# Adding the key bias on GpSimd instead of by a matmul, with GpSimd's batch laid out in steps

## What is computed

```python
xn = layernorm(x)
Q, K, V = xn @ Wq.T + bq, xn @ Wk.T + bk, xn @ Wv.T + bv
Q, K = elu(Q) + 1, elu(K) + 1
KV = einsum('bshd,bshe->bhde', K, V);  K_sum = K.sum(axis=1)
Z = 1 / (einsum('bshd,bhd->bsh', Q, K_sum) + 1e-6)
out = einsum('bshd,bhde,bsh->bshe', Q, KV, Z) @ Wo.T + bo
return x + out + ffn(xn)
```

## Time and profile before

| | us |
|---|---|
| median of three runs | 1902.34 (1901.63 to 1903.81) |
| the profiled execution, its own time | 1900.01 |
| its span, first to last instruction | 1898.3 |
| PE busy | 1863.2 (98%) |
| DVE busy | 1300.6 (69%) |
| ACT busy | 1272.2 (67%) |
| POOL busy | 1026.2 (54%) |

### The profile page before, as it was taken

The page is one execution under the profiler, slowest core; times in us unless marked ns, Lnnn a source line. Parts: engine busy times, 40 slices in busy tenths (PEclk is TensorE's granted clock), DMA queues, the critical chain, the costliest instruction groups (busy, mean ns, idle before and its releaser), DMA issues. The chain is left out here.

```text
span 1898.3 us, 38991 instructions
## 1 busy us (share of the span) xinstructions
PE 1863.2 (98%) x13562; PEld 1269.6 (67%) x13562; DVE 1300.6 (69%) x2611; ACT 1272.2 (67%) x2045; POOL 1026.2 (54%) x947
## 2 busy tenths in 40 slices
PE   6899999999999999999999999999999999999998
PEld 4566666666676666666666666666666666666666
DVE  6678999998857777655787875555555555555556
ACT  6988887777746666666666666666666666666664
POOL 5656565656445555654455455545554554555453
PEclk9999999999999999999999999999999999999999
DMA  6979897989675555666677667576766766676857
GB/s 174 231 221 247 216 251 240 225 236 254 190 191 132 122 120 123 148 179 150 165 157 181 154 158 183 135 177 151 192 152 160 169 143 180 155 187 154 183 120 223
DMA packets 448900, 338.22 MB, mean 178 GB/s; under 512 B 224757, under 2 KB 430330, under 8 KB 448762
## 3 DMA queue, kind: packets, MB, share of 16 engines
q1 hardware_dynamic: 383674, 253.84, 48.5%
q0 software_dynamic: 48864, 66.88, 19.8%
q10 hardware_dynamic: 16224, 15.73, 2.5%
HBM read 185.61 MB, written 100.40 MB: 151 GB/s over the span
## 5 line engine op out<-in xcount | busy, mean ns | idle before, releaser
L1961 PE MATMUL pY<-w2s,hid 128*128 128x256 f16 x6144 | 756.6, 273 | 0.8 <-DVE hid L1806 0.8
L1946 PE MATMUL pH<-xgT,w1s 128*128 128x512 f16 (+1 forms) x3120 | 747.7, 376 | 1.3 <-PEq L324 1.3
L1961 PEld LDWEIGHTS pY<-w2s,hid 128*128 128x128 f16 x6144 | 599.8, 98 | 180.6 <-DVE yo L1822 3.6
L1806 DVE SCALAR_TENSOR_TENSOR hid<-gel,cur,hid 128x512 f16<-128x512 f32 (+1 forms) x520 | 384.6, 740 | 446.4 <-ACT hid L1745 440.8
L1720 POOL DMA_INDIRECT acc<-yo,idx x254 | 405.9, 1598 | 523.0 <-DVE yo L1822 450.0
L1742 ACT ACTIVATE gel<-pH,cur 128x512 f32<-128x512 f32 (+1 forms) x520 | 353.8, 680 | 476.7 <-PE pH L1946 457.2
L1946 PEld LDWEIGHTS pH<-xgT,w1s 128*128 128x128 f16 x3120 | 305.1, 98 | 252.4 <-DMA xgT<-xg 1.6
L1745 ACT ACTIVATE hid<-gel,cur 128x512 f16<-128x512 f32 (+1 forms) x520 | 372.0, 715 | 17.1
L219 POOL DMA_INDIRECT xg<-table,idx x256 | 286.1, 1118 | 112.1 <-issue 58.2
L1270 PE MATMUL pP<-wkv,xT 128*128 128x512 f16 x768 | 201.8, 381 | 7.8 <-DVE bias_rows L981 4.7
L724 POOL TENSOR_SCALAR xm<-xring,moments 128x256 f32<-128x256 f32 x128 | 120.9, 954 | 72.3 <-DVE xhl L1002 72.2
(11 more groups left out here) (236 smaller groups left out, 1888.5 us busy)
## 6 DMA issues: line engine op xcount, KB each, us to landing
stage<-in_w SPq DMA_DIRECT2D x160, 512.0 KB, 6.4
xring<-in_x SPq DMA_DIRECT2D x16, 1024.0 KB, 6.4
x2ring<-in_x SPq DMA_DIRECT2D x16, 1024.0 KB, 7.6
table<-xhl SPq DMA_DIRECT2D x32, 512.0 KB, 4.1
mix<-x2ring SPq DMA_DIRECT2D x32, 512.0 KB, 3.0
acc<-zeros SPq DMA_DIRECT2D x16, 1024.0 KB, 4.6
fmix<-mix SPq DMA_DIRECT2D x48, 256.0 KB, 3.5
facc<-acc SPq DMA_DIRECT2D x48, 256.0 KB, 4.0
```

The source lines that it names most:

```text
L1806: v.scalar_tensor_tensor(out=hid[:, hc % 4, 1, w], in0=gel[:, hc % 2, w], scalar=cur[expert_of(b, q)][:, 1:2], in1=hid[:, hc % 4, 0, w], o ...
L1946: last = t.matmul(pH[hc % 4][:, tok], w[:, aw, c, hc * P:(hc + 1) * P], xgT[i][:, ad, c, tok], start=k == 0 and c == 0, stop=k == 2 and c ...
L1961: last = t.matmul(pY[s // 2][:, s % 2, :], hid[:, hc % 4, ad, s * P:(s + 1) * P], w[:, aw, hc, :], start=hc == 0 and k == 0 and s % 2 == 0 ...
```

## The change

The product L1273 is left out for tiles 0 to 6 of each batch and kept for tile 7. A new constant `bk_all` holds the key bias in all partitions, made once by a product into `pG` and an ACT copy. For tiles 0 to 6, `keys` only copies the bank into `kv1`; POOL then adds `bk_all` to the keys there (`add_bk`, event `k_biased`); after that ACT makes `ek` from `kv1` (`key_exp`, relu and exponential), at the end of its step. POOL's list of a batch is written in eight steps that begin with `add_bk(n, j)`. DVE's list is unchanged. `bo_row` moves into a free part of `x2ring`, and the making of two constants is split off (`spread_consts`).

```diff
+            bk_all = sb("bk_all", [P, D], F32)
...
+                def add_bk(n, j):
+                    if n == 0 and j == 0:
+                        pool.wait_ge(whi, at(whi, 0, 6))
+                    pool.wait_ge(kv_done, at(kv_done, n, j))
+                    g.tensor_tensor(kv1[:, j % 4, 0:DC, 0:P], kv1[:, j % 4, 0:DC, 0:P],
+                                    bk_all[:, :].rearrange("p (c t) -> p c t", c=DC), ALU.add).then_inc(k_biased, 1)
...
                 for n in range(NB):
-                    for j in range(HALF, NT):
-                        centre(n, j)
-                    if n >= LAG:
-                        for u in range(4):
-                            add_bo(n - LAG, u)
-                    if n < NB - 1:
-                        norm(n + 1)
-                        for j in range(HALF):
-                            centre(n + 1, j)
-                    if n == 0:
-                        later_consts()
-                    if n + 1 >= LAG:
-                        blocks_of(n + 1 - LAG)
+                    s2, nxt = n >= LAG, n < NB - 1
+                    for j in range(NT):
+                        if n == 0 and j < HALF:
+                            centre(0, HALF + j)
+                        if j < NT - 1:
+                            add_bk(n, j)
+                        if s2 and j < 2:
+                            add_bo(n - LAG, 2 * j)
+                            add_bo(n - LAG, 2 * j + 1)
+                        if nxt and j == (3 if n == 0 else 2):
+                            norm(n + 1)
+                        if nxt and j == 3:
+                            for i in range(HALF - 1):
+                                centre(n + 1, i)
+                        if nxt and j == 4:
+                            centre(n + 1, HALF - 1)
...
+                        if n + 1 >= LAG and j == 4:
+                            scale_bv(n + 1 - LAG)
+                        if n + 1 >= LAG and j == 5:
+                            blocks_of(n + 1 - LAG)
+                        if nxt and j > 5:
+                            centre(n + 1, 2 * j - 8)
+                            centre(n + 1, 2 * j - 7)
...
+                def key_exp(n, j):
+                    if j < NT - 1:
+                        act.wait_ge(k_biased, at(k_biased, n, j))
+                        act.wait_ge(k_done, at(k_done, n, j - 2))
+                        a.activation(ek[:, j % 2, :].rearrange("p (c t) -> p c t", c=DC), kv1[:, j % 4, 0:DC, 0:P],
+                                     ACT.Relu, scale=-1.0).then_inc(kneg_done, 1)
...
-                            if k == 0 and c == 0:
+                            if j == NT - 1 and k == 0 and c == 0:
```

More of the change, by code:

```diff
@@ L350, in block_program @@
             bqT = sb("bqT", [P, DC], F32)
-            bo_row = sb("bo_row", [1, D], F32)
+            bo_row = x2ring[0:1, 1, 2, :]
             rows_all = sb("rows_all", [P, 2 * D], F32)
@@ L445, in block_program @@
             bias_step = event("bias_step")
+            k_biased = event("k_biased", per=NT - 1)
             lhs_done = event("lhs_done")
@@ L737, in blocks_of @@
                         g.tensor_scalar(kvm[:, c, :], bv_all[:, c * P:(c + 1) * P], kvs[:, c, P:P + 1], None, ALU.mult).then_inc(kvb_done, 1)
+                def blocks_of(m):
+                    kvs = kvring[:, m % QR, :, :]
                     for c in range(DC):
@@ L754, in _ @@
                 for n in range(NB):
[L755 to L767 removed]
+                    s2, nxt = n >= LAG, n < NB - 1
[14 more added lines that the diff above has]
+                            centre(n + 1, HALF - 1)
+                        if n == 0 and j == 4:
+                            later_consts()
+                        if n == 0 and j == 5:
+                            spread_consts()
+                        if n + 1 >= LAG and j == 4:
[5 more added lines that the diff above has]
+                            centre(n + 1, 2 * j - 7)
                 for u in range(4):
                     add_bo(NB - LAG, u)
+                scale_bv(NB - 1)
                 blocks_of(NB - 1)
@@ L792, in weights_high @@
                     a.activation(rows_all[:, :], pKV[:, :], ACT.Copy).then_inc(whi, 1)
+                    a.activation(bk_all[:, :], flat(pG)[:, 0:D], ACT.Copy).then_inc(whi, 1)
                 def high(n, j):
@@ L805, in keys @@
                     act.wait_ge(proj, at(proj, n, j))
-                    act.wait_ge(k_done, at(k_done, n, j - 2))
-                    a.activation(ek[:, j % 2, :], pP[j % 2][:, 0:D], ACT.Relu, scale=winv_neg[:, 2:3]).then_inc(kneg_done, 1)
+                    if j == NT - 1:
+                        act.wait_ge(k_done, at(k_done, n, j - 2))
+                        a.activation(ek[:, j % 2, :], pP[j % 2][:, 0:D], ACT.Relu, scale=winv_neg[:, 2:3]).then_inc(kneg_done, 1)
                     act.wait_ge(kv_used, at(kv_used, n, j - 4))
@@ L863, in _ @@
                         keys(n, j)
+                        if j == NT - 1:
+                            key_exp(n, j)
                         if nxt and j == NT - 2:
@@ L1258, in _ @@
                 pe.wait_ge(b_in, at(b_in, 0, 6))
+                t.matmul(flat(pG)[:, 0:D], ones[0:1, :], bias_raw[0:1, 0:D], start=True, stop=True)
                 t.matmul(pKV[:, 0:D], ones[0:1, :], bo_row[:, :], start=True, stop=True)
```

5 lines of the change are left out of this document (4 added, 1 removed).

## The result

The changed kernel takes 2002.76 us (median of 4 runs, 2000.92 to 2004.91), the kernel before 1902.74 beside it (1901.63 to 1903.81): ratio 1.0528, 95% interval 1.0515 to 1.0541. The profiled execution took 2000.92, its span is 1999.1 us, 100.8 longer than before. By the last `denominators` of the attention stage (625.47 us against 525.73) 99.7 of it have arisen.

What follows compares the result with a forecast made beforehand. The prediction took PE as the bound, with next to no slack between division and output. It added 69 us (batches 2 to 14), 1 (batch 15) and 10 (batches 0 to 2) to 1900.01: 1980 us, range 1945 to 2010.

Steps and rivals of the forecast that it cites:

- What the change removes, 12 us: On PE, 112 fewer bias products at 0.10 to 0.11 us: 0.75 us a batch, if PE never waits longer.
- The add, 0.75: On POOL, each 128x256 add taken as 0.75 us, between bounds 0.46 and 1.36; 5.3 us a batch fit POOL's room.
- Startup: Before the batches, one small product and ACT copy, taken as nothing; batches 0, 1 and 2's late begin together: 10 us.
- The walk: Batch 8's chain through POOL, ACT, DVE and PE: output starts 5.6 us late, rounded to 5.3 a batch; chance 0.59.
- I count it apart, as a rival: DVE stopped by POOL's SBUF reads, left out of the chain because the lost time would fall into DVE's idle time.
- no edge of this kind is left: From `output(m, 0)` to the next batch, 14.5 us of PE work: adds of tiles 5 and 6 have over 5 us.
- once 1.31: DVE's 32-element subtraction, median 0.22 us, took 1.31 once, just when POOL's `add_bo` of 1.36 began.
- The second: Rival: full chain, and PE's clock falls in its waits, slowing output work; 1.5 us a batch, 2000 us; chance 0.14.
- The fourth: Rival: DVE becomes the bound, each add blocking it for 0.75; period 33.8 us, time 1926 to 1930; chance 0.03.
- The first: Rival: shorter chain, ACT and POOL reach tile 2 no later; output 3.2 us late, 1945 us; chance 0.15.
- third: Rival: PE stays the bound, both divisions end by 278.2 in batch 8, whole 12 us gained: 1888 us; chance 0.07.
- fifth: Rival: no change within 0.2%, a wait that happens to cost just the gain; chance 0.02.

Runs made afterwards that it cites:

- run 3: The kernel before without the bias product for tiles 0 to 6 and nothing in its place, their key bias left out: 1893.34 us, ratio 0.9962.
- run 12: The changed kernel with two POOL memsets, still waited for, in place of each add; key bias of tiles 0 to 6 left out: 1991.82 us, ratio 1.0465.
- run 11: The kernel before, product kept, POOL's list in steps, with two memsets that nobody waits for in each add's place: 1924.63 us, ratio 1.0121.
- run 8: The changed kernel with logits and divisions earlier on DVE, POOL's list by due times, and ACT's tile 4 `ek` ahead of its `rstd` wait: 1948.66 us.
- run 9: As run 8, with DVE's root, second query feature and top-k parts 1 to 4 moved behind the divisions: 1923.54 us, ratio 1.0119.
- run 5: The changed kernel with `norm` of the next batch moved from step 2 to step 3, behind the add of tile 3: 2012.35 us, ratio 1.0596.
- runs 2: The kernel before, product kept, POOL's list in steps, with 112 same-size adds on an unread constant that nobody waits for: 1944.3 us, ratio 1.0232.
- run 7: The changed kernel with only DVE's list altered: gate logits ahead of tile 3's `k_feature`, three divisions ahead of tile 4's: 1977.29 us, ratio 1.0397.

## Why the prediction was right, and what it missed

The sign and the mechanism were right and the time lies inside the range, but the size was short by 23 us (1980 against 2002.76), of which 20.9 against the profiled execution's 2000.92. These 20.9 are divided up below.

- *What the change removes, 12 us.* The product costs what was said, but run 3 gives 8. The step took PE to be the only bound, though the text itself had found the edge of division and output to have next to no slack.
- *The add, 0.75.* Its median is 0.73 (716 to 1275 ns, mean 768). Startup: batch 2 begins 10.6 late, 10 had been taken. Batch 15: 1.2 for 1.
- *The walk.* Times of batch 8 less 49.50, with the walk's in brackets: add of tile 1 at 267.45 (267.3), `ek` of tile 1 at 269.07 (269.05), `ek` of tile 2 at 273.14 (273.3). Then `k_feature` of tile 2 at 274.49 (273.4), and from there everything keeps the distance: gate 281.40 (its logits 280.2), output 285.51 (284.4). `norm` took 2.80 (2.8), the three centres 3.06 (2.9).
- *The step that failed* is "I count it apart, as a rival, because DVE's lost time would fall into its new idle time". The idle time comes behind the moments; the lost time lies ahead of them, where DVE works without a gap. In batch 8, `ek` of tile 2 was ready at 322.64, but DVE came to it at 323.99. Against the kernel before, DVE is 3.51 later there, counted from `denominators`. Of these, 2.27 are longer instructions between the first `stats` behind `denominators` and `k_feature` of tile 2 (10.13 for 7.86), mainly `xhl` and `k_feature` of tile 0. The other 1.24 DVE brings along: it begins those `stats` 1.29 after `denominators` instead of 0.05, after it stood 5.08 in step 6. The prediction had "no edge of this kind is left" there. No run takes these two parts apart; in batches 2 to 5 the `stats` come at most 0.3 after `denominators`, and the output starts at 20.8 to 21.9 instead of 22.4.
- *Its size.* Over batches 2 to 14 the output starts 22.12 after `denominators` on average against 15.90, 6.22 more where 5.3 had been taken: 12.0 us of the 20.9. The choice to round the chain down from 5.6 is 4 of these, DVE's lateness the other 8. In run 12, without the adds' reads, the output comes at 21.33, 0.79 earlier. The Trainium skill (SBUF — State Buffer, Who interferes with whom) was right in both directions: run 11 has GpSimd busy as long without reading, and its writes lengthen nothing. The rows had said more than the prediction took from them: its "once 1.31" stands for 12 of the 32 executions of `gsub` in the trace before, which take 1.31 to 1.32.
- *Behind the output* the prediction had nothing lost. The mean stretch from output to the next `denominators` is 38.59 - 22.12 = 16.47 against 31.90 - 15.90 = 16.00, 6.1 us in 13 batches, though a batch at full clock needs only 15.74 (batch 12). That is 0.22 less than the usual 15.96 of before, two products: tile 6's, and that of the next batch's tile 0, which the prediction didn't count here. The 0.73 from 15.74 to 16.47, 9.5 us in all, are the clock: in 9 of 13 batches the output's first eight products run partly at the lower level, 3.66 instead of 1.97 in batch 8.
- *The rivals.* The second (clock, 2000) named the number that came nearest, in part by luck. Its fall is real: in the 9 batches it came after waits of 3.4 to 4.3 us, and by that the trace agrees with the Trainium skill (TensorE: Matmul & The Clock Gate, Loop structure matters more than you think). But it was priced at 1.5 a batch and costs 0.73; the rest of the way to 2000 is DVE's. The slow time is in part absorbed by the wait in front of the output (in batch 12 all of it: 0.50 from 489 to 492, the output at 492.16 at full clock). The fourth (DVE blocked, period 33.8) didn't decide here, but once the queues are repaired its number is near: 34.12 on average in run 8, 34.5 in batch 8. DVE isn't full there either, it stands 1.2 and 3.1 for `ek` of tiles 5 and 6; what has no gap is its way to the divisions. The first, third and fifth fell with the periods of 36.6 to 40.0.
- *Sum.* Predicted 69 + 10 + 1 = 80; measured 86.9 + 10.6 + 1.2 = 98.7, plus 1.1 between the last two `denominators` and 1.1 behind them. So 12.0 on the chain, 6.1 behind it, 0.7 at the ends and 2.2 elsewhere were missing, by rounding 0.1 more than the 20.9.

What stays open: heard and unheard parts don't simply add. Hearing costs 67 us with memsets (1924.6 to 1991.8) and 58 with adds (1944.3 to 2002.8), and each of these includes what the missing product gives back. What the 11.0 us at the start of run 9 are made of stays open too. Batch 2 begins 10.6 late in the changed kernel, and no run repairs the order of batches 0 and 1.

## What to carry to other kernels

An engine with 40% of its time free isn't free where work is handed through its queue: write down what stands ahead of the new instruction in the list, what that waits for, and whether the thing waited for depends on the new instruction itself, as `norm` of the next batch did through `k_feature` and the moments. A new wait also shifts all that is queued behind it, so ask which instructions of the other engines it will now run beside. To repair such a move, lists on both sides have to change together: moving one item (run 5) only moved the wait and cost more clock, while due times on POOL and room on DVE brought back 79 of 101 us, for a product whose removal was worth 8.

## What the runs showed of the hardware

- The exclusion lengthens both sides. POOL's power of 128x8 takes 1.67 us in most batches of the kernel before and has a mean of about 2.35 in runs 2 and 11, where it runs beside DVE's `q_feature` and `k_feature`. On DVE, the first cast of 128x128 has a median of 0.23 before and 0.98 in run 8, and the `tensor_scalar` of 128x8 (`rstd`) 0.18 in run 11 and 0.69 in run 8: instructions with a single input are held too.
- Two memsets of POOL with a wait between cost 0.31 + 0.06 + 0.31 = 0.68, about as long as an add (0.72), and no instruction of DVE that runs beside them alone is lengthened (run 11: `rstd` 0.18 nine times, `k_feature` 0.41 to 0.43 six times).
- PE's clock stood at 1.00 while PE waited (327 to 331) and fell after it, when PE was at work again: 0.81 from 331 to 332, 0.50 from 332 to 338. In batch 4, where PE waited 1.57 for the gate and 2.10 for the output, the output's products took the full-clock 1.97. A short wait doesn't always leave the clock whole: in run 7, with 1.86 in front of the output, the same products took 2.92 to 2.96 in batches 5 to 13.
